# Attention scores in three PSUM banks with one exponential per head, in a fused AdaLN block on one core

## What is computed

```python
q = _apply_rotary(q, rope)
k = _apply_rotary(k, rope)
scale = HD ** (-0.5)
scores = jnp.einsum('bhqd,bhkd->bhqk', q, k) * scale
causal_mask = jnp.triu(jnp.ones((Tx, Tx), dtype=bool), 1)
scores = jnp.where(causal_mask, -jnp.inf, scores)
attn = jax.nn.softmax(scores, axis=-1)
out = jnp.einsum('bhqk,bhkd->bhqd', attn, v)
...
x = x + ga * _L0_attn_ref(h, L0_attn_qkv_w, ...)
h = _layernorm(x, axis=-1) * (1 + cb) + sb
x = x + gb * _L0_ffn_ref(h, L0_ffn_gate_w, ...)
```

## Time and profile before

| | us |
|---|---|
| median of 3 runs (3038.55 to 3047.42) | 3045.78 |
| the profiled execution | 3040.35 |
| its span, first to last instruction | 3038.6 |
| PE busy | 2802.9 |
| DVE busy | 2287.0 |
| ACT busy | 1781.1 |
| POOL busy | 1254.0 |
| attention loop, first to last exponential | 346.7 to 2105.5 |
| mean granted clock | 0.975 |

### The profile page before, as it was taken

How to read it: one execution, slowest core, us unless ns; L and a number is a source line. 1 busy time by engine, 2 the same in 40 slices (tenths; PEclk the granted TensorE clock), 3 DMA queues, 4 the chain that set the end, 5 groups by cost and what they waited for, 6 DMA issues and landing times.

```text
span 3038.6 us, 57895 instructions
## 1 busy us (share of the span) xinstructions
PE 2802.9 (92%) x20452; PEld 1452.4 (48%) x20452; DVE 2287.0 (75%) x6063; ACT 1781.1 (59%) x2736; POOL 1254.0 (41%) x1557
## 2 busy tenths in 40 slices
PE   7788799999999999989998999987999999999997
PEld 4433222223322223322223322223888899999996
DVE  7888799998889998899998889922492225665477
ACT  3322367666566766656665567675566666666532
POOL 6756311123521114511113865554305744443176
PEclk9999799999999999999999999999999999999998
DMA  4853323223312332321323424245336756665486
GB/s 164 214 140 102 108 59 67 65 46 76 103 39 56 67 65 64 103 50 30 66 59 91 141 93 130 89 133 158 116 94 212 238 193 184 180 187 171 139 238 191
DMA packets 288762, 358.85 MB, mean 118 GB/s; under 512 B 63484, under 2 KB 241292, under 8 KB 288220
## 3 DMA queue, kind: packets, MB, share of 16 engines
q1 hardware_dynamic: 259516, 279.94, 33.7%
q0 software_dynamic: 26112, 71.34, 7.5%
q10 hardware_dynamic: 2848, 3.87, 0.5%
HBM read 206.25 MB, written 139.21 MB: 114 GB/s over the span
## 4 chain that ended last, share of the span: by engine, by line
PE 44%; DVE 16%; ACT 12%; POOL 8%; issue 7%; DMA 1%; ACTq 0%; POOLq 0%; SPq 0%; DVEq 0%
ACT P L1641 12%; PE PB L1161 11%; PE PB L1177 7%; DVE mx L1457 7%; PE PB L1088 7%; PE PB L1039 5%; PE PB L1058 5%; PE PB L1071 5%; POOL x_slots L1843 4%; DVE PB L1454 4%; PE PB L1146 2%; PE PB L1102 2%; POOL yg L1856 1%; PE PB L1125 1%; POOL x_slots L1835 1%
## 5 line engine op out<-in xcount | busy, mean ns | idle before, releaser
L1641 ACT ACTIVATE P<-PB 128x1024 f32<-128x1024 f32 (+3 forms) x1280 | 1097.8, 894 | 619.7 <-PE PB L1071 615.6
L1457 DVE TENSOR_REDUCE mx<-PB 128x1 f32<-128x512 f32 x1536 | 975.0, 683 | 116.6 <-PE PB L1039 110.1
L1039 PE MATMUL PB<-KO,QO 64*128 64x512 bf16 (+3 forms) x2560 | 771.8, 356 | 75.7 <-DVE mx L1457 39.3
L1088 PE MATMUL PB<-P,V 128*17 128x512 f32 (+3 forms) x5120 | 599.8, 541 | 10.1 <-POOL P L1794 9.9
L1058 PE MATMUL PB<-QO,KO 64*128 64x512 bf16 (+3 forms) x2560 | 544.7, 355 | 61.3 <-ACT P L1641 34.7
L1039 PEld LDWEIGHTS PB<-KO,QO 64*128 64x128 bf16 x2560 | 206.2, 94 | 781.2 <-DVE mx L1457 358.9
L1454 DVE CUSTOM_DVE_ANT_0 PB<-PB,mk 128x128 f32<-128x128 f32 (+3 forms) x1024 | 481.7, 510 | 44.5 <-PE PB L1039 41.8
L1071 PE MATMUL PB<-QO,KO 34*128 34x512 bf16 (+3 forms) x2560 | 504.3, 353 | 0.1
L1794 POOL TENSOR_SCALAR_AFFINE_SELECT P<-P 128x256 f32<-128x256 f32 x512 | 207.9, 412 | 654.7 <-ACT P L1641 649.2
L1161 PE MATMUL PB<-xT,ws 128*128 128x128 f32 x3432 | 432.5, 276 | 5.6 <-ACT xT L1723 5.4
L1161 PEld LDWEIGHTS PB<-xT,ws 128*128 128x128 f32 x3432 | 406.9, 193 | 8.4 <-ACT xT L1723 8.4
(11 more groups left out here) (174 smaller groups left out, 3099.2 us busy)
## 6 DMA issues: line engine op xcount, KB each, us to landing
xq<-x_slots SPq DMA_DIRECT2D x286, 128.0 KB, 2.9
qk_parts<-pt SPq DMA_DIRECT2D x192, 128.0 KB, 2.4
KO<-qk_parts SPq DMA_DIRECT2D x192, 128.0 KB, 4.0
y_slots<-yo SPq DMA_DIRECT2D x191, 128.0 KB
QO<-qk_parts SPq DMA_DIRECT2D x64, 256.0 KB, 3.5
rden<-rden_rows SPq DMA_DIRECT2D x256, 64.0 KB
y_slots<-mx SPq DMA_DIRECT2D x95, 128.0 KB
v_rows<-vst SPq DMA_DIRECT2D x16, 544.0 KB, 4.0
```

Of the source, the lines that this page charges most:

```text
L1039: mm = pe.matmul(PB[:, bank, 0:n], QO[half, k3, j, 128 * t:128 * t + 128], KO[half, k3, j, 512 * kc:512 * kc + n], start=True, stop=True)
L1088: mm = pe.matmul(PB[32 * j:32 * j + 17, 7, c0:512], V[:, g % 2, kt, 17 * j:17 * j + 17], P[:, pbuf(g, i, j // 2), j % 2, 0:n], start=kt == ...
L1457: dve.tensor_reduce(mx[:, j, t, kc:kc + 1], PB[:, u.bank[item], 0:n], AX.X, ALU.max).then_inc(s["mx"], 1)
L1641: act.activation(P[:, pbuf(g, i, p), :, 0:n], PB[:, 2 * p:2 * p + 2, 0:n], ACT.Exp, scale=0.25).then_inc(s["exp"], 1)
```

## The change

Scores go into three banks, one head each, in turn: head number 4 x step + j takes bank (4 x step + j) mod 3. There is one exponential per head, on half the elements, 2560 in all. Max units and projection pieces have four banks, 3 to 6. The mask on diagonal steps stays one instruction per pair, after the pair's second exponential. The order of a step's items is new: PV moves from the step's start to its end, the pieces of `pumped` behind it, and the `sa` of the next step's first two heads stand right behind the `sb` of head 2.

```diff
--- before.py
+++ after.py
...
@@ -231,7 +232,7 @@
-    u.banks = [4, 5, 6]
+    u.banks = [3, 4, 5, 6]
...
@@ -340,27 +342,29 @@
         quota = (want - done) // 2 * 2
         at = done
         ahead = order[n + 1] if n + 1 < len(order) else None
-        if len(pend) == 2:
-            values(*pend.pop(0))
+        o("sa", g, i, 2)
+        o("sa", g, i, 3)
         maxima(at + (quota + 2) // 4)
-        o("sa", g, i, 3)
-        o("sa", g, i, 2)
         maxima(at + quota // 2)
+        o("sb", g, i, 2)
         if ahead:
             o("sa", *ahead, 0)
             o("sa", *ahead, 1)
+        o("exp", g, i, 2)
         o("sb", g, i, 3)
-        o("sb", g, i, 2)
-        o("exp", g, i, 1)
+        o("exp", g, i, 3)
+        if ahead:
+            o("sb", *ahead, 0)
+            o("exp", *ahead, 0)
+        maxima(at + quota // 2 + (quota + 2) // 4)
+        maxima(at + quota)
+        if ahead:
+            o("sb", *ahead, 1)
+            o("exp", *ahead, 1)
+        if len(pend) == 2:
+            values(*pend.pop(0))
         if i >= 2:
             pumped(pumps)
-        maxima(at + quota // 2 + (quota + 2) // 4)
-        if ahead:
-            o("sb", *ahead, 0)
-            o("sb", *ahead, 1)
-        maxima(at + quota)
-        if ahead:
-            o("exp", *ahead, 0)
         send_rows()
         if i == 38:
             flat_turns()
...
@@ -618,6 +622,13 @@
         def chunk(g, i):
             return 4 * g + STEPS[i][0]
 
+        def sbank(g, i, j):
+            return (4 * (40 * g + i) + j) % SB
+
+        def sbank_before(g, i, j):
+            k = 4 * (40 * g + i) + j - SB
+            return None if k < 0 else (k // 4 // 40, k // 4 % 40, k % 4)
+
         def pbuf(g, i, p):
             return (2 * (40 * g + i) + p) % NP
 
...
@@ -1048,14 +1059,15 @@
                 elif name == "sa":
                     g, i, j = at
                     c, kt = STEPS[i]
-                    k3, p = (g + 2) % 3, j // 2
+                    k3 = (g + 2) % 3
                     n, c0 = nb(i)
                     q0 = 512 * c + c0
                     rows = slice(64 * (j % 2), 64 * (j % 2) + 64)
                     q.wait_ge(s[f"l_g{k3}"], 16 * NL * (g // 3 + 1))
-                    if o.n("exp", g, i, p) > 2:
-                        q.wait_ge(s["exp"], o.n("exp", g, i, p) - 2)
-                    pe.matmul(PB[:, j, 0:n], KO[rows, k3, j, 128 * kt:128 * kt + 128], QO[rows, k3, j, q0:q0 + n],
+                    before = sbank_before(g, i, j)
+                    if before is not None:
+                        q.wait_ge(s["exp"], o.n("exp", *before))
+                    pe.matmul(PB[:, sbank(g, i, j), 0:n], KO[rows, k3, j, 128 * kt:128 * kt + 128], QO[rows, k3, j, q0:q0 + n],
                               start=True, stop=False).then_inc(s["sa"], 1)
                 elif name == "sb":
                     g, i, j = at
...
@@ -1151,6 +1163,9 @@
                     q.wait_ge(s["xT"], n + 1)
                     if n >= 2:
                         q.wait_ge(s["ha"], n - 1)
+                    else:
+                        for wait in done_before:
+                            q.wait_ge(*wait)
                     q.wait_ge(s["routed"], p + 1)
                     q.wait_ge(s["l_ew"], 16 * 2 * len(W_PARTS))
                     if kind == "x":
...
@@ -1632,13 +1647,13 @@
                     q.wait_ge(s["lo_g"], n_lo["g"])
                     q.wait_ge(s["w_mod"], 16)
                 elif name == "exp":
-                    g, i, p = at
+                    g, i, j = at
                     n, c0 = nb(i)
-                    q.wait_ge(s["st"], 2 * o.n(*item))
-                    before = pbuf_before(g, i, p)
+                    q.wait_ge(s["st"], o.n("sb", g, i, j))
+                    before = pbuf_before(g, i, j // 2)
                     if before is not None:
                         q.wait_ge(s["pv"], o.n("pv", *before))
-                    act.activation(P[:, pbuf(g, i, p), :, 0:n], PB[:, 2 * p:2 * p + 2, 0:n], ACT.Exp, scale=0.25).then_inc(s["exp"], 1)
+                    act.activation(P[:, pbuf(g, i, j // 2), j % 2, 0:n], PB[:, sbank(g, i, j), 0:n], ACT.Exp, scale=0.25).then_inc(s["exp"], 1)
                 elif name == "nrows":
                     g, p = at
                     k3 = (g + 2) % 3
...
@@ -1787,9 +1802,9 @@
                     q.wait_ge(s["utri"], 1)
                     pool.affine_select(out=utri[:, :], in_=onesb[:, :], compare_op=ALU.is_gt, fill=0.0, base=0, pattern=[[1, 128]],
                                        channel_multiplier=-1).then_inc(s["utri"], 1)
-                elif name == "exp" and diag(at[1]):
-                    g, i, p = at
-                    k = pbuf(g, i, p)
+                elif name == "exp" and diag(at[1]) and at[2] % 2:
+                    g, i, j = at
+                    k = pbuf(g, i, j // 2)
                     q.wait_ge(s["exp"], o.n(*item))
                     pool.affine_select(out=P[:, k, :, 0:128], in_=P[:, k, :, 0:128], compare_op=ALU.is_ge, fill=0.0, base=0,
                                        pattern=[[0, 2], [1, 128]], channel_multiplier=-1).then_inc(s["cut"], 1)
```

More of the change, by code:

```diff
@@ L34 @@
 OWN = 5
+SB = 3
 STEPS = [(c, kt) for c in range(4) for kt in range(4 * c + 4)]
@@ L323, in plan @@
     order = [(g, i) for g in range(16) for i in range(40)]
-    o("sa", 0, 0, 0)
-    o("sa", 0, 0, 1)
-    o("sb", 0, 0, 0)
-    o("sb", 0, 0, 1)
-    o("exp", 0, 0, 0)
+    for j in (0, 1):
+        o("sa", 0, 0, j)
+    for j in (0, 1):
+        o("sb", 0, 0, j)
+    for j in (0, 1):
+        o("exp", 0, 0, j)
     pumps = []
@@ L656, in program @@
                 scat_exp[tuple(at)] = n_exp - 1
-            if name == "exp" and diag(at[1]):
+            if name == "exp" and diag(at[1]) and at[2] % 2:
                 n_cut += 1
-                o.nth["cut"][tuple(at)] = n_cut
+                o.nth["cut"][at[0], at[1], at[2] // 2] = n_cut
             if name == "lo":
@@ L1080, in _ @@
                         else:
-                            q.wait_ge(s["exp"], o.n("exp", g, i, p))
+                            q.wait_ge(s["exp"], o.n("exp", g, i, 2 * p + 1))
                     q.wait_ge(s[f"l_v{g % 2}"], 16 * (g // 2 + 1))
@@ L1143, in _ @@
                     else:
-                        q.wait_ge(s["exp"], 1280)
+                        q.wait_ge(s["exp"], 2560)
                     for f in (0, 1):
```

## The result

The changed kernel takes 3405.48 us (median of 4 runs, 3400.12 to 3407.21) beside 3042.16 for the kernel before on the same chip: ratio 1.120, 95% interval 1.118 to 1.121. The forecast was 3290. The sign and the main wait were right, the size was not: +363 us measured, +245 forecast, and the time lies just above the range's upper end. The profiled execution has a span of 3398.3 us at a mean granted clock of 0.959.

What follows compares the result with a forecast made beforehand. A loop through PE and ACT (scores to exponential to bank), not DVE, bounds the full step. Group terms, less 5 for POOL and plus 5 for the clock, gave +245 on 3040.4: 3285, stated as 3290 us; range 3195 to 3400.

Steps and rivals of the forecast that it cites:

- POOL: Attention loop: PV a step later gives the masks on POOL more room, taken as 5 us less.
- PE stands there for the whole way out and back: `sa` of next head 1 waits for exponential 2: 1.10 us from `sb` 2, full step 3.29 us.
- No second wait.: Full step: `sa` 3 at 2.84 finds exponential 0 done at 2.64, `sa` 0 at 3.29 exponential 1 at 3.14.
- sb 2 to sb 2 is 1.10 + 1.515 + 0.225 = 2.84: Full step of the last group, without maxima: 2.84 us against 2.67 before, +6 us for the group.
- Clock +5: PE's clock already falls for a few windows in the kernel before; 5 us added to the sum.
- Rival 1: PE's clock falls in the loop: one step in ten +140 us, 3430; one in thirty +47, 3335; chance 0.15.
- Projection at 35 us a batch: Groups with projection: its pieces stand behind PV as PE time of their own, 35 us per batch kept.
- Exponentials per head: ACT needs 2.08 us per full step, before 1.94, below any step time; by itself costs nothing.
- Fourth bank: DVE may fall up to four results behind; removes PE's short waits for DVE, already left out of 118.4 us a group.
- Rivals 2 to 4: PE's wait half hidden, 3165 (0.06); DVE the bound, within 10 us of before (0.03); faster, 2975 (0.04).
- A plain pair of groups near 237 us: Sign of being right: two groups without projection or routing take near 237 us, before 198.2 to 200.5.
- last group little changed: Sign of being right: the last group, which has no maxima, changes little; +6 us in the sum.

Runs made afterwards that it cites:

- the kernel with `sa` 0 three times: Changed kernel with head 0's `sa` matmul issued three times in every step, same operands and bank, result unchanged: 3358.1 us, ratio 1.106 to the kernel before.

## Why the prediction was right and wrong

What each group was to add and what it added, in us (profiled executions, group times as in the table above):

| groups | forecast | measured |
|---|---|---|
| 0 | +14 | +30.6 |
| 1, 2 / 5, 6 / 13, 14 (plain) | +38.6 / +38.1 / +36.3 | +46.5 / +46.7 / +46.7 |
| 3, 4 / 7, 8 / 11, 12 (projection) | +38.6 / +34.4 / +20.7 | +39.8 / +38.6 / +27.3 |
| 9, 10 (routing) | +18.4 | +27.5 |
| 15 | +6 | +57.5 |
| POOL, clock | -5, +5 | in the rows above |
| sum | +245 | +361 |

- *"PE stands there for the whole way out and back", 1.10 us, full step 3.29.* Right: 1.07, 3.27, and one for one with the exponential's length. With it came three steps that failed, the next three points.
- *"No second wait."* Wrong. It was worked out for a step with a 512-wide PV and then used for all. There `sa` 3 stood 0.20 us behind the end of exponential 0 (2.84 and 2.64), and a narrow PV brings it forward by 0.42 or 0.64. Behind a narrow PV I had 2.84 and 2.62 us for a full step (2.19, plus 0.645 or 0.425); in six such steps of a group it took 3.12 and 3.11, which is 2.3 us a group. A plain group became 121.6 in place of 118.4; the rest of that lies in the other steps.
- *Last group, "sb 2 to sb 2 is 1.10 + 1.515 + 0.225 = 2.84".* The worst term: +6 became +57.5. I left out the two pairs of maxima, ahead of `sb` 2 and of `sb` 1, and thought their time saved, but each `sb` follows its own `sa` by 0.45 with or without them: full steps there are 3.27 at full clock, and 5.00 at the lower one. The 0.43 us in each of 28 full-width steps are some 12 us (an estimate); the rest of the 51 missed goes, by this reckoning, with the 95 us at low clock, and the kernel with `sa` 0 three times gives back 23.
- *Clock +5.* It was 42 to 47 us. Rival 1 was right in kind. That its price for one step in thirty is 47 too is luck: a full step at the lower clock costs 1.73 us more and not 2.2, and half of the low-clock time is in one group. I looked for it in the steady loop, where it hardly happened, and not in the group where PE has least to do beside its waits.
- *Projection at 35 us a batch.* In groups 3 and 4 the forecast, +38.6 against +39.8, was near because two errors offset: two plain groups take 243.2 us and not 236.8, and projection adds 30.3 and not 35. The first group's +30.6 in place of +14 went with 40 us at low clock, before 12; no run takes it apart.
- *Exponentials per head "by itself costs nothing".* Under the stall I know nothing against it; on the kernel before, without the stall, it costs 1.0%. *Fourth bank:* the waits for DVE that it was to remove are not there in plain groups of the changed kernel with three banks for maxima either.
- *Rivals 2 to 4* did not occur: the stall was whole, and DVE did not bound the full step.
- *My signs.* PE's idle 0.69 us before `sa`, the step of 3.27 and the exponential of 0.60 came as said. "A plain pair of groups near 237 us" (243.2) and "last group little changed" (161.1 after 103.6) failed.

The range missed by 5 us. Its upper end came from half of the clock rival; the second wait, once ruled out, was no bound in it.

Left open: what keeps the clock low for 65 us in the last group once a 1.87 us wait has brought it down, and how much of the 18 us with three maxima banks is the clock's.

## What to carry to other kernels

Count the banks in flight along the engine's program order: a bank that is asked for again one instruction pair after it was filled makes the engine stand for the whole way through the other engine and back, and one PSUM bank of 8 was worth 11% here. Having found one wait, work the loop out again for every width of the step and for steps in which the work beside it is missing; the next loop was only 0.16 us behind here. Where PE must wait and its clock falls, matmuls that hide in the wait are worth trying: 1280 of them saved 42 to 47 us here.

## What I had not expected of the hardware

An `sb` into a bank starts 0.45 us after the `sa` into the same bank that its semaphore waits for, at 512 columns and full clock, where nothing else holds it up (in all traces but once never less than 0.43), though the next independent pair goes after 0.22. Four exponentials of 128 columns take 0.79 us in a row, 0.19 more than one of 512.
